# First router of a four-layer gated network: choosing four experts of sixteen with largest-eight and replace-first-match instructions per token tile

## The chip, the cores and the metric

One core of one Trainium2 chip. The metric is the device time of one execution in microseconds (us), as the median of several runs. Engines are called PE (TensorE, matrix multiplication), PEld (its weight loads), DVE (VectorE), ACT (ScalarE), POOL (GpSimd) and SP (SyncE, which here only issues DMA).

## The reference, cut to what matters

The network has four layers, each a cross-attention part and a feed-forward part, on 4 x 256 tokens of width 256. The change touches the router of the first layer's feed-forward part, a mixture of 16 experts in 4 groups. Per token, the two best groups are kept (a group's score is the sum of its two best biased scores), the four best experts in those groups are chosen, and their unbiased scores, normalised, become the weights:

```python
logits = x @ gate_weight.T
scores = jax.nn.sigmoid(logits)
biased = scores + expert_bias[None, :]
grp = biased.reshape(T, N_GROUP, gsz)                  # 4 groups of 4
top2, _ = jax.lax.top_k(grp, 2)
_, gidx = jax.lax.top_k(top2.sum(-1), TOPK_GROUP)      # 2 groups
gmask = jax.nn.one_hot(gidx, N_GROUP).sum(1)
masked = jnp.where(jnp.repeat(gmask, gsz, axis=1) > 0, biased, -jnp.inf)
_, sel = jax.lax.top_k(masked, TOP_K)                  # 4 experts
w = jnp.take_along_axis(scores, sel, axis=1)
w = w / (w.sum(-1, keepdims=True) + 1e-20) * SCALING
```

The experts' outputs (silu(x g) * (x u)) d are then summed with these weights, and a shared expert is added.

## The kernel before, in words

The 1024 tokens are 8 tiles (NT) of 128; a tile's tokens lie on the 128 partitions. All engines run programs of their own (the blocks at the end of `flamingo`), which meet at named semaphores. The order of the work is written out by hand; there is no planner. The stages are: the first state-space layer (`mamba0_*`), its tail, a layer norm (`ln_*`, k=1), the softplus that prepares the second state-space layer (`softplus_vector`, l=1), the first router (`router_*`, r=0), then one loop over the 8 token tiles in which the 17 units of the first mixture (`ffn_*`, f=0) are interleaved with the second state-space layer's scan (`mamba1_*`), then the ternary feed-forward part, the third layer's attention (`attn2_*`), an fp8 feed-forward part, the fourth attention, the second router and its experts.

Around the change:

- PE turns the normalised tokens (L328), ACT copies them to ZT (L336), PE multiplies them with the gate weights (L1058) and ACT takes the sigmoid (L1070) into `sc`, 128 x 128 (8 tiles of 16 experts).
- DVE meanwhile runs `softplus_vector` for l=1 (L457 to L481). Only behind it, in its own program's order, does it begin `router_vector`. Each of the router's instructions goes through `link`, which makes the instruction raise a semaphore and DVE wait for it before it starts the next.
- `router_vector` adds the bias (L1099), scores the groups (L1105 to L1113), picks two groups by the helper `top_k` with n=4 (the first of its two calls), writes a very low number (-3e38) over the experts of the other groups (L1118 to L1121), picks four experts by `top_k` with n=16 (the second call, with which the diff is concerned), and turns the chosen scores into the weights `cw` (L1123 to L1129). The last instruction raises `cw_done`.
- `top_k` compares all pairs: for every value it counts those that are larger, or equal and further in front, and takes the values whose count is below k. That is five instructions on 128 x (8 n n) elements: equal (L1084), times a mask (L1085), greater (L1086), add (L1087), reduce (L1089), and a comparison of the 8 n counts with k (L1090). For n=16 the five have 2048 elements per partition, for n=4 128.
- In `ffn_gpsimd` POOL waits for `cw_done`, then copies the first tile's tokens (L733) and weights (L737), and then starts the scan's products (`mamba1_drive`, L674). PE waits for these two copies before the first tile's matmuls (L782); ACT (L814) waits for PE, and DVE (L847, L850) for ACT. The same loop's scan on DVE is L643, its products with C are L651 and POOL's sums L681.
- SP has by then issued, in this order: the weights `gu0` and `dn0`, the ternary weights (L1969), the tables `moe` (L1970), `slot_scratch` (L1971, 4 MB), and the first four rows of the second scan (L350), which wait for nothing of the router. Further rows (L350) wait for the loop's own progress.

Of the kernel before, what the change touches and what calls it, by code (L numbers as in the profile page):

```python
# [7 lines left out]
ALU = mybir.AluOpType  # L8
# [11 lines left out]
NT = TOK // P  # L20
# [9 lines left out]
NEXP = 16  # L30
# [67 lines left out]
def flamingo(nc, a, out):  # L98
    with ExitStack() as ctx:
# [32 lines left out]
        def col(name):  # L132
            at, w = COL_AT[name]
            return cols[:, at:at + w]
# [155 lines left out]
        def S(name):  # L290
            if name not in sems:
                sems[name] = sem(name)
            return sems[name]
# [770 lines left out]
        sc, bi, sel, tmp1, tmp2, rank, grp, sm = (z[:, k * n_te:(k + 1) * n_te] for k in range(8))  # L1064
# [10 lines left out]
        def top_k(link, v, n, k, into):  # L1075

            a3 = v.rearrange("p (t i) -> p t i", t=NT)
            vi = a3.rearrange("p t (i o) -> p t i o", o=1).to_broadcast([P, NT, n, n])
            vj = a3.rearrange("p t (o j) -> p t o j", o=1).to_broadcast([P, NT, n, n])
            size = NT * n * n  # L1080
            c1 = cmp1[:, 0:size].rearrange("p (t i j) -> p t i j", t=NT, i=n)
            c2 = cmp2[:, 0:size].rearrange("p (t i j) -> p t i j", t=NT, i=n)
            before = jlti.rearrange("p (o i j) -> p o i j", o=1, i=NEXP)[:, :, 0:n, 0:n].to_broadcast([P, NT, n, n])
            link(nc.vector.tensor_tensor(c1, vj, vi, ALU.is_equal))  # L1084
            link(nc.vector.tensor_tensor(c1, c1, before, ALU.mult))  # L1085
            link(nc.vector.tensor_tensor(c2, vj, vi, ALU.is_gt))  # L1086
            link(nc.vector.tensor_tensor(c1, c1, c2, ALU.add))  # L1087
            rk = rank[:, 0:NT * n]
            link(nc.vector.tensor_reduce(rk.rearrange("p (t i) -> p t i", t=NT), c1, AX.X, ALU.add))  # L1089
            link(nc.vector.tensor_scalar(into, rk, float(k), None, ALU.is_lt))  # L1090

        def router_vector(dve, link, r):
            t3 = lambda v, n=NEXP: v.rearrange("p (t e) -> p t e", t=NT)
            nu = FFN[0 if r == 0 else 3]["units"]
            if r == 0:
                link(nc.vector.memset(cw[:], 0.5))
                dve.wait_ge(S("scores"), 1)
                eb = col("ebias").rearrange("p (o e) -> p o e", o=1).to_broadcast([P, NT, NEXP])
                link(nc.vector.tensor_tensor(t3(bi), t3(sc), eb, ALU.add))  # L1099

                g = bi.rearrange("p (q k) -> p q k", k=4)
                q4 = [g[:, :, k] for k in range(4)]
                n4 = n_te // 4
                m1, n1, m2, n2 = (tmp1[:, k * n4:(k + 1) * n4] for k in range(4))
                link(nc.vector.tensor_tensor(m1, q4[0], q4[1], ALU.max))  # L1105
                link(nc.vector.tensor_tensor(n1, q4[0], q4[1], ALU.min))
                link(nc.vector.tensor_tensor(m2, q4[2], q4[3], ALU.max))
                link(nc.vector.tensor_tensor(n2, q4[2], q4[3], ALU.min))
                link(nc.vector.tensor_tensor(n1, n1, n2, ALU.max))
                link(nc.vector.tensor_tensor(n2, m1, m2, ALU.min))  # L1110
                link(nc.vector.tensor_tensor(n1, n1, n2, ALU.max))
                link(nc.vector.tensor_tensor(m1, m1, m2, ALU.max))
                link(nc.vector.tensor_tensor(grp[:, 0:n4], m1, n1, ALU.add))  # L1113
                gsel = grp[:, n4:2 * n4]
                top_k(link, grp[:, 0:n4], 4, 2, gsel)

                em = gsel.rearrange("p (q o) -> p q o", o=1).to_broadcast([P, n4, 4])
                link(nc.vector.tensor_tensor(bi.rearrange("p (q k) -> p q k", k=4), g, em, ALU.mult))  # L1118
                link(nc.vector.tensor_scalar(grp[:, 2 * n4:3 * n4], gsel, 1.0, BIG, ALU.subtract, ALU.mult))
                pen = grp[:, 2 * n4:3 * n4].rearrange("p (q o) -> p q o", o=1).to_broadcast([P, n4, 4])  # L1120
                link(nc.vector.tensor_tensor(bi.rearrange("p (q k) -> p q k", k=4), g, pen, ALU.add))  # L1121
                top_k(link, bi, NEXP, 4, sel)
                link(nc.vector.tensor_tensor(tmp2, sc, sel, ALU.mult))  # L1123
                link(nc.vector.tensor_reduce(sm[:, 0:NT], t3(tmp2), AX.X, ALU.add))
                link(nc.vector.tensor_scalar(sm[:, 0:NT], sm[:, 0:NT], 1e-20, None, ALU.add))
                link(nc.vector.reciprocal(sm[:, NT:2 * NT], sm[:, 0:NT]))
                link(nc.vector.tensor_scalar(sm[:, NT:2 * NT], sm[:, NT:2 * NT], 0.5 * 2.5, None, ALU.mult))
                rc = sm[:, NT:2 * NT].rearrange("p (t o) -> p t o", o=1).to_broadcast([P, NT, NEXP])
                nc.vector.tensor_tensor(cw[:, :, 0:NEXP], t3(tmp2), rc, ALU.mult).then_inc(S("cw_done"), 1)  # L1129
# [951 lines left out]
        def _(dve):  # L2081
# [11 lines left out]
            softplus_vector(dve, link, 1)  # L2093
            dve.wait_ge(S("ld_w0"), 80)
            router_vector(dve, link, 0)
            ffn_vector(dve, 0, link)
            ln_vector(dve, link, 2)
# [125 lines left out]
```

## Time and profile before

| | us |
|---|---|
| median of 3 runs | 1041.7 |
| the runs | 1047.06, 1041.70, 1039.58 |
| the profiled execution, its own time | 1044.17 |
| its span in the profile | 1042.4 |
| mean granted TensorE clock in it | 0.869 of full |

The span is from the first to the last recorded instruction; the execution's own time is 1.8 us longer. In the profile an instruction is named by its line in the kernel (L1084), its engine, its operation, and output <- input by the program's names. PEclk is the TensorE clock that was granted, as a share of full speed.

### The profile page before, as it was taken

What the parts mean: (1) busy time and instruction counts of PE and PEld (TensorE: products, weight loads), DVE (VectorE), ACT (ScalarE), POOL (GpSimd) and SP (SyncE); (2) the same over time, 40 slices, a digit from 0 to 9 for tenths busy, and PEclk for the clock granted to TensorE, in tenths of its full rate; (3) what the DMA queues carried; (4) which work ended last, traced back from release to release, by engine and by line L of the source; (5) the groups of instructions that cost most, each with busy time, mean ns of one, the idle gap of its engine ahead of it and who ended that gap; (6) DMA issues with size and microseconds to landing.
All of it is one profiled execution on the core that took longest, in us unless ns stands there. A gap on an engine that the chain in (4) does not pass through costs nothing.

```text
span 1042.4 us, 12920 instructions
## 1 busy us (share of the span) xinstructions
PE 839.0 (80%) x4202; PEld 528.8 (51%) x4202; DVE 698.1 (67%) x1136; ACT 390.9 (37%) x824; POOL 417.0 (40%) x295
## 2 busy tenths in 40 slices
PE   5887898850688899888489887999884886979993
PEld 2332333340566777677377544555543675645661
DVE  5995999979788889888766554667845546412222
ACT  1433222340334444443255542465550531103331
POOL 4005666400466666666239602333520242232331
PEclk8985888975799999999789896899997996889997
DMA  5102212763022221221020011314126001051114
GB/s 206 45 1 108 74 60 81 282 219 88 0 81 81 81 81 43 78 80 40 0 72 1 31 61 40 119 33 134 34 65 221 12 1 61 22 189 64 46 49 149
DMA packets 28099, 81.67 MB, mean 78 GB/s; under 512 B 3313, under 2 KB 17153, under 8 KB 26529
## 3 DMA queue, kind: packets, MB, share of 16 engines
q1 hardware_dynamic: 25648, 73.25, 20.7%
q0 software_dynamic: 2256, 6.18, 1.7%
q10 hardware_dynamic: 144, 1.57, 0.4%
q8 instruction: 31, 0.51, 0.2%
q14 instruction: 20, 0.16, 0.1%
HBM read 65.64 MB, written 17.35 MB: 80 GB/s over the span
## 4 chain that ended last, share of the span: by engine, by line
PE 47%; DVE 18%; issue 15%; POOL 11%; DMA 3%; ACT 3%; SPq 1%; DVEq 0%; POOLq 0%; ACTq 0%
PE ps L511 6%; POOL M L674 4%; PE ps L1686 4%; PE ps L1327 4%; PE ps L1690 3%; PE ps L390 3%; PE ps L504 3%; PE ps L1728 3%; PE ps L894 2%; DVE M L643 2%; POOL ZT L977 2%; PE ps L1346 2%; DVE M L651 2%; POOL slot_scratch L1212 1%; PE ps L1604 1%
## 5 line engine op out<-in xcount | busy, mean ns | idle before, releaser
L782 PE MATMUL ps<-W,F 128*128 128x256 f32 x544 | 152.3, 406 | 54.4 <-POOL F L737 33.0
L782 PEld LDWEIGHTS ps<-W,F 128*128 128x128 f32 x544 | 103.2, 199 | 86.6 <-DVE W L850 39.5
L585 POOL TENSOR_TENSOR M<-M 128x1024 f32<-128x1024 f32 x32 | 75.2, 2352 | 100.6 <-DVE M L465 53.6
L681 POOL TENSOR_TENSOR W<-W,M 128x1024 f32<-128x1024 f32 x32 | 75.4, 2356 | 84.5 <-DVE M L651 84.5
L1757 ACT ACTIVATE N<-ps 128x512 f32<-128x512 f32 x128 | 69.5, 595 | 86.6 <-PE ps L1690 86.6
L814 ACT ACTIVATE F<-ps 128x128 f32<-128x128 f32 x136 | 37.7, 277 | 149.7 <-PE ps L782 149.6
L643 DVE TENSOR_TENSOR_SCAN M<-ps,M 128x512 f32<-128x512 f32 x64 | 78.0, 1219 | 21.4 <-POOL M L674 21.4
L1686 PE MATMUL ps<-M,W 32*128 32x256 f32 x512 | 78.8, 443 | 16.3 <-DVE W L1784 11.1
L1778 DVE TENSOR_REDUCE W<-ps 128x4 f32<-128x1024 f32 x64 | 78.1, 1221 | 12.5 <-PE ps L1690 9.2
L769 PE MATMUL ps<-W,F 128*128 128x256 f32 x272 | 83.8, 391 | 0.0
L1690 PE MATMUL ps<-W,M 32*128 32x256 f32 x512 | 83.8, 424 | 0.0
L511 PE MATMUL ps<-M,ident 128*128 128x512 f32 x128 | 75.0, 740 | 5.6 <-DVE M L610 5.6
L601 DVE TENSOR_TENSOR_SCAN M<-ps,M 128x1024 f32<-128x1024 f32 x32 | 73.3, 2290 | 8.4 <-ACT ps L556 5.3
L674 POOL TENSOR_TENSOR M<-N,M 128x1024 f32<-128x1024 f32 x32 | 74.9, 2349 | 0.0
L1686 PEld LDWEIGHTS ps<-M,W 32*128 32x128 f32 x512 | 47.5, 205 | 44.6 <-DVE W L1784 25.0
L556 ACT ACTIVATE ps<-M 128x1020 f32<-128x1020 f32 x32 | 35.7, 1115 | 81.7 <-DVE M L601 81.7
L894 PE MATMUL ps<-N_rounded,W_rounded 128*128 128x512 f32 x224 | 56.4, 397 | 3.2 <-DVE N_rounded L878 3.2
L1420 POOL DMA_INDIRECT ytok_scratch<-Z,M x31 | 29.7, 958 | 71.7 <-ACT Z L1382 71.7
L967 POOL TENSOR_TENSOR M_rounded<-Z,M_rounded 128x512 fp32r<-128x512 f32 x28 | 40.4, 1445 | 43.1 <-ACT M_rounded L944 43.1
L1690 PEld LDWEIGHTS ps<-W,M 32*128 32x128 f32 x512 | 56.2, 197 | 2.7 <-issue 1.2
L511 PEld LDWEIGHTS ps<-M,ident 128*128 128x128 f32 x128 | 28.6, 235 | 53.1 <-issue 42.2
L1399 DVE COPY M<-ps 128x128 f32<-128x128 f32 x31 | 9.1, 292 | 66.0 <-PE ps L1337 66.0
(279 smaller groups left out, 1723.8 us busy)
## 6 DMA issues: line engine op xcount, KB each, us to landing
M<-dbl_scratch SPq DMA_DIRECT2D x48, 512.0 KB, 4.0
W<-in_gu SPq DMA_DIRECT2D x1, 4800.0 KB, 16.2
W<-in_gu SPq DMA_DIRECT2D x1, 4352.0 KB, 14.4
att_scratch<-W SPq DMA_DIRECT2D x32, 128.0 KB
slot_scratch<-in_slots SPq DMA_DIRECT2D x1, 3999.0 KB, 18.7
M<-slot_scratch SPq DMA_DIRECT2D x3, 1032.0 KB, 9.4
W<-in_gu SPq DMA_DIRECT2D x2, 1536.0 KB, 6.9
W<-in_dn SPq DMA_DIRECT2D x1, 2176.0 KB, 19.1
```

Source lines behind the costliest of these rows:

```text
L511: last = nc.tensor.matmul(ps[:, 2 * t + half, :], ident[:], hC[:, t, half * HALF:(half + 1) * HALF], start=(n == 0), stop=True, skip_group ...
L585: nc.gpsimd.tensor_tensor(dBu[:, t, :], du[0][:, t, :], Bb[:, par, :], ALU.mult).then_inc(S("dBu_rdy"), 1)
L601: nc.vector.tensor_tensor_scan(hst[:, t, :], dAp, dBu[:, t, :], 0.0, ALU.mult, ALU.add).then_inc(S("h_rdy"), 1)
L643: nc.vector.tensor_tensor_scan(hst[:, t, at], dAp1[:, at], dBu[:, t, at], 0.0, ALU.mult, ALU.add).then_inc(S("h1_rdy"), 1)
L674: nc.gpsimd.tensor_tensor(dBu[:, t, :], du[1][:, t, :], Bb[:, par, :], ALU.mult).then_inc(S("dBu1_rdy"), 1)
L681: nc.gpsimd.tensor_tensor(u[1][:, t, :], u[1][:, t, :], hC[:, t, :], ALU.add).then_inc(S("y1_acc"), 1)
L769: last = nc.tensor.matmul(ps[:, YBANK[par], 0:DIM], hT[0:k, c % 4, :], dn[0:k, c, :], start=(c == 0), stop=(c == nch - 1))
L782: last = nc.tensor.matmul(up, ztt[:, par, c, :], gu[:, c, s, :], start=(c == 0), stop=(c == DC - 1))
L894: last = nc.tensor.matmul(ps[:, 4 + 2 * kind + q % 2, :], gu[:, c, u, kind * P:(kind + 1) * P], part[:, c, half * HALF:(half + 1) * HALF], ...
L1686: return nc.tensor.matmul(ps[:, b, q * SEQ:(q + 1) * SEQ], qst[32 * b:32 * b + 32, h, q * P:(q + 1) * P], kst[32 * b:32 * b + 32, h, :], s ...
L1690: return nc.tensor.matmul(ps[:, 4 + n % 3, k * SEQ:(k + 1) * SEQ], kst[32 * b:32 * b + 32, e, k * P:(k + 1) * P], qmax[32 * b:32 * b + 32, ...
L1778: nc.vector.tensor_reduce(spots[:, 2 * which:2 * which + 2], ps[:, 2 * which:2 * which + 2, :].rearrange("p b (q k) -> p b q k", q=2), AX. ...
```

## The change

The second call of `top_k` (n=16, k=4) goes. In its place DVE finds, for each of the 8 token tiles, the eight largest of the 16 scores (`max`, output in falling order, in `best`). After the last of them one memset overwrites the fifth to eighth of each with 2.5e38, which no score equals. Then, for each tile, `match_replace` looks for the eight numbers of `best` among the 16 scores and writes 3.0e38 over the first place at which each is found, into `tmp1`. A comparison with 3.0e38 gives `sel`. Within each group of eight instructions there is no wait; DVE waits after the last max, after the memset, after the last match_replace and after the comparison. The group router's `top_k` (n=4) and everything else stay.

```diff
+        TAKEN, NEVER = 3.0e38, 2.5e38
...
-                top_k(link, bi, NEXP, 4, sel)
+                best = rank[:, 0:8 * NT].rearrange("p (t k) -> p t k", t=NT)
+                for t in range(NT):
+                    last = nc.vector.max(best[:, t, :], t3(bi)[:, t, :])
+                link(last)
+                link(nc.vector.memset(best[:, :, 4:8], NEVER))
+                for t in range(NT):
+                    last = nc.vector.match_replace(t3(tmp1)[:, t, :], best[:, t, :], t3(bi)[:, t, :], TAKEN)
+                link(last)
+                link(nc.vector.tensor_scalar(sel, tmp1, TAKEN, None, ALU.is_equal))
```

## Rows read from the trace of the kernel before

**Rows 1.** The page: span, busy time, slices, and the chain that ended last.

```profile
span 1042.4 us, 12920 instructions
PE 839.0 (80%) x4202; PEld 528.8 (51%) x4202; DVE 698.1 (67%) x1136; ACT 390.9 (37%) x824; POOL 417.0 (40%) x295
...
PE 47%; DVE 18%; issue 15%; POOL 11%; DMA 3%; ACT 3%; SPq 1%; DVEq 0%; POOLq 0%; ACTq 0%
```

**Rows 2.** Waits, 235 to 269 us: engine, line, waited for, total us, times, longest.

```profile
POOL F L733 <- DVE F L1129: 42.4, 1, 42.4
...
PE ps L782 <- POOL F L737: 33.0, 1, 33.0
```

**Rows 3.** Timeline 225 to 300 us: start, duration, engine, line, operation, shape.

```profile
254.37 2.29 DVE L1084 TENSOR_TENSOR M<-Z 128x2048 f32<-128x2048 f32 x1
256.69 2.29 DVE L1085 TENSOR_TENSOR M<-M,F 128x2048 f32<-128x2048 f32 x1
...
263.67 2.29 DVE L1089 TENSOR_REDUCE Z<-M 128x128 f32<-128x2048 f32 x1
265.99 0.23 DVE L1090 TENSOR_SCALAR Z<-Z 128x128 f32<-128x128 f32 x1
...
267.55 0.29 DVE L1129 TENSOR_TENSOR F<-Z 128x128 f32<-128x128 f32 x1
268.02 0.39 POOL L733 COPY F<-ZT 128x256 f32<-128x256 f32 x1 [42.40 <-DVE F L1129]
...
268.61 5.32 PE L782 MATMUL ps<-W,F 128*128 128x256 f32 x12 [33.02 <-POOL F L737]
```

**Rows 4.** Chain that ended last, by line, 247 to 272 us.

```profile
by line: POOL M L674 18.4%; DVE M L1084 10.4%; DVE M L1087 10.4%; DVE M L1085 10.4%; DVE M L1086 10.4%; DVE Z L1089 10.4%; issue 6.3%; DVE N L465 4.9%; DVE Z L1090 1.7%; POOL F L733 1.6%; DVE Z L1099 1.2%; DVE F L1129 1.2%; DVE Z L1123 1.2%
```

**Rows 5.** Stretches: window, length, busy (x) of PE, PEld, DVE, ACT, POOL, PEclk, DMA share, GB/s.

```profile
244.00:248.00 4.00, 0.00 (x0) 0.00 (x0) 3.86 (x5) 0.00 (x0) 0.00 (x0) 0.50 0.14 58
...
256.00:260.00 4.00, 0.00 (x0) 0.00 (x0) 3.93 (x3) 0.00 (x0) 0.00 (x0) 0.50 0.00 0
...
268.00:272.00 4.00, 3.39 (x8) 2.71 (x9) 0.64 (x2) 1.20 (x2) 3.98 (x4) 0.50 0.00 0
...
276.00:280.00 4.00, 3.98 (x20) 3.08 (x20) 3.89 (x10) 2.07 (x7) 0.79 (x1) 1.00 0.00 0
```

**Rows 6.** Groups of DVE instructions: one small one by line, and a run of eight.

```profile
222.90 0.64 DVE L309 BATCH_NORM_AGGREGATE mv<-stats 128x2 f32<-128x6 f32 x8
...
L309 DVE BATCH_NORM_AGGREGATE mv<-stats x56: 146/149/183, 13.1 to 876.5; 128x2 f32<-128x6 f32 x56
...
L481 DVE MEMSET ps<- x1: 62/62/62, 248.8 to 248.8; 128x4 f32 x1
L1096 DVE MEMSET F<- x1: 178/178/178, 249.0 to 249.0; 128x144 f32 x1
...
L1111 DVE TENSOR_TENSOR Z<-Z 128x32 f32<-128x32 f32 x1 | 0.2, 193 | 0.0
```

**Rows 7.** Groups of instructions of the whole span: busy us, mean ns of one.

```profile
L1804 DVE RECIPROCAL M<-M 128x256 f32<-128x256 f32 x8 | 14.0, 1745 | 18.7 <-DMA M<-att_scratch 18.7
L1784 DVE TENSOR_TENSOR W<-ps,W 128x256 f32<-128x256 f32 x32 | 13.5, 423 | 28.3 <-PE ps L1718 28.3
```

**Rows 8.** Timeline of DVE in the third layer's attention: one L1784 per round.

```profile
636.54 0.42 DVE L1784 TENSOR_TENSOR W<-ps,W 128x256 f32<-128x256 f32 x1 [1.09 <-PE ps L1718]
642.55 0.42 DVE L1784 TENSOR_TENSOR W<-ps,W 128x256 f32<-128x256 f32 x1 [2.15 <-PE ps L1718]
...
659.54 0.42 DVE L1784 TENSOR_TENSOR W<-ps,W 128x256 f32<-128x256 f32 x1 [2.38 <-PE ps L1718]
663.48 0.43 DVE L1784 TENSOR_TENSOR W<-ps,W 128x256 f32<-128x256 f32 x1 [0.95 <-PE ps L1718]
```

**Rows 9.** Stretches there (columns as in rows 5).

```profile
639.00:642.00 3.00, 3.00 (x21) 1.60 (x15) 1.23 (x1) 1.15 (x3) 0.00 (x0) 0.50 0.00 0
...
660.00:663.00 3.00, 3.00 (x44) 1.91 (x40) 2.32 (x2) 1.44 (x4) 0.32 (x1) 1.00 0.02 7
```

## The prediction

> **What bounds the kernel now.** I began with the page, to see whether one engine is the bound: none is. PE is busy 80% of the span and makes 47% of the chain that ended last, DVE 18%, POOL 11% [rows 1]. So what a change is worth depends on its stage. Next I asked for the waits around the first router. Three engines stand still there. POOL waits 42.4 us, in one piece, for the router's last instruction (L1129), and PE waits 33.0 us for the copy that POOL makes behind it [rows 2]. ACT's next unit of the mixture needs PE. Nothing else than DVE runs: in the windows at 244, 256 us PE, ACT and POOL are at 0.00, and from 256 us the DMA moves nothing [rows 5]. The timeline then shows what DVE does in this hole. Behind the softplus of the second scan, which takes up to 249 us, it works through the router one linked instruction at a time. Five of them, on 2048 elements a partition, fill 254.37 to 265.99 us: L1084 to L1087 and L1089, at 2.29 us each [rows 3]. The chain confirms that they set the end: each of these five lines holds 10.4% of the stretch from 247 to 272 us, that is 2.6 us (2.3 us for the wide one, the rest for the narrow one of the group router) [rows 4]. The chance that any of this is hidden is therefore small.
>
> **What goes.** From the start of the wide L1084 (254.37) to the start of the comparison L1090 behind it (265.99) are 11.62 us [rows 3]: five times 2.29, and the gap of 0.03 us with which each linked instruction follows the last (256.69 - 254.37 - 2.29). The comparison stays in another form, one pass over 128 elements like L1090, 0.23 us [rows 3], so it cancels. The group router keeps its six narrow instructions.
>
> **What comes.** The trace has no max and no match_replace, so I price them by rows of small DVE instructions.
> - Price of an element: 128x32 takes 0.193 us [rows 6], 128x2048 takes 2.29 us [rows 3]; that is 2.10 us over 2016 elements, 1.04 ns each, and a fixed part of 0.16 us.
> - Price when several stand in a row without a wait, as here: eight of L309 take 0.64 us together, though one alone lasts 0.149 us [rows 6]. So they follow each other at (0.64 - 0.15) / 7 = 0.07 us: most of the fixed part overlaps.
> - Eight max: each reads 16 and writes 8 elements where L309 reads 6 and writes 2. I allow 0.02 us for that (16 elements at 1.04 ns): 7 x 0.09 + 0.17 = 0.80 us.
> - The memset writes 32 elements: between 0.06 us for 4 and 0.18 us for 144 [rows 6], 0.09 us.
> - Eight match_replace: the call must first take in eight values and then run over 16. I count two passes, 0.08 + 0.09 = 0.17 us: 7 x 0.17 + 0.26 = 1.45 us.
> - Three waits (after the last max, the memset, the last match_replace) at 0.03 us: 0.09 us.
>
> Sum 0.80 + 0.09 + 1.45 + 0.09 = 2.43 us, against 11.62: a gain of 9.2 us.
>
> The ends of that unknown. Below: match_replace is one pass and all run at L309's pace, 0.64 + 0.64 + 0.06 + 0.09 = 1.4 us, gain 10.2. Above: the dearest DVE arithmetic in the trace is the reciprocal, 1745 ns for 256 elements against 423 ns for a product of the same shape [rows 7], 5.2 ns more each. If the search for eight values went at 1.04 + 5.2 = 6.2 ns an element and nothing overlapped, an instruction on 16 elements would take 0.16 + 0.10 = 0.26 us; 24 of them and the memset and waits make 6.4 us, gain 5.2. I take the value near the lower end, because L309 is the nearest row: tiny, on the same engine, issued eight in a row without a wait.
>
> A rule that speaks against this: the Trainium skill, page "VectorE: DVE Perf Modes", section "The DRAIN you can't avoid", says that a DVE instruction starts only when the pipe behind the last is empty, that leaving out semaphores does not help, and that one should reduce the number of operations. This change raises the number. By that rule the eight L309 would have to take 8 x 0.149 = 1.2 us and take 0.64 [rows 6], so this trace does not bear it out for tiny instructions; the same page's section "Two Vector instructions with no wait between them" allows an earlier start, and counts match_replace as two instructions, which is what I had assumed. What the full price of each would give is worked out as a rival below from rows alone.
>
> **What is late next.** With cw ready 9.2 us earlier, at about 258.7 us, POOL's copies (L733), the scan's first product (L674) and PE's first matmul (L782) must find their other inputs. The tokens ZT and the gate products are done at 236 us, since PE stands still from then on (33.0 us before 268.61) [rows 2, 3]. The rows and weights that DMA brings are all issued before, wait for nothing of the router, and traffic is down to 58 GB/s in the window at 244 us and to 0 in the one at 256 us [rows 5]. No later DMA is issued until the loop asks for it. Apart from DVE I find nothing that is due between 249 us and 258 us, so the whole 9.2 us should reach the first matmul. The loop behind it is the same work and moves forward as a block; its rows are fetched on its own progress and move with it.
>
> The clock: PE begins the loop at half speed (1.2 GHz) in the window at 268 us and is at full speed (2.4 GHz) in the one at 276. It is at half speed already at 244 us, 8 us after PE's last work [rows 5]. A hole of 24 us in place of 33 therefore still ends at half speed, and the rise costs the same.
>
> **The sum.** The profiled execution took 1044.17 us (span 1042.4 [rows 1] and 1.8 outside it); 1044.17 - 9.2 = 1035.0 us. That execution lies 2.5 us above the median of the runs, 1041.7. The saving does not depend on that, so for a median I predict 1041.7 - 9.2 = 1032.5 us, 0.9% less. The three runs of before lie between 1039.6 and 1047.1, so a median of a few is good to some 3 us, and about 1% is what such a measurement can tell from no change. My forecast lies just inside it.
>
> **The rivals.**
> 1. *No overlap.* Each of the new instructions pays its whole 0.16 + 0.02 us: 24 x 0.18 + 0.18 = 4.5 us, gain 7.1, 1034.6 us. For it: max and match_replace need all eight comparisons finished, so they may not run into each other as L309's do. Against: L309's spacing [rows 6]. Chance 0.20.
> 2. *The clock falls elsewhere, to our good.* The moments at which TensorE's clock drops in later stages move with the work. In the third layer's attention a round (L1784 to L1784) takes 642.55 - 636.54 = 6.01 us at half speed and 663.48 - 659.54 = 3.94 us at full speed [rows 8, 9]. If the three slow rounds there went at full speed, 6.2 us more would be gained: 1026.3 us. The spread of the runs of before, 7.5 us, says that something of this size happens anyway. Chance 0.17.
> 3. *The clock falls elsewhere, to our harm, and it is slower.* The same mechanism, the other way: each further round at half speed in that attention costs 2.07 us. From 9.2 / 2.07 = 4.4, so five more slow rounds, the gain is gone; with nine it is 18.6 - 9.2, 1051.1 us. For it: there are 32 rounds, and most now run at full speed. Against: it needs some 30 us more at half speed in a stage in which PE hardly pauses once it has the full clock, and the work ahead of it is the same. Chance 0.03.
> 4. *Another wait takes the router's place.* A row of the scan or a table lands later than I read it, and POOL or PE still starts near 268 us: 1041.7 us. Rows 5 speak against it (no traffic at 256 us). Chance 0.04.
> 5. Forecast, overlapping small instructions with the later stages as they are: 0.56.
>
> **How the numbers follow.** The likeliest is 1032.5 us. The unknown price puts it between 1031.5 (gain 10.2) and 1036.5 (gain 5.2); the median's own uncertainty widens this to some 1029 and 1039, and rival 2 pulls the lower end down to 1027. Range 1027 to 1039. Faster by over 1% means below 1031.3: about a quarter of the forecast's 0.56, nearly all of rival 2, a little of rival 1, 0.34 together. Slower by over 1%: rival 3, 0.03. Within 1%: the rest, 0.63.
>
> **What would show it right or wrong.** In the profile of the changed kernel: the lines of `top_k` appear once each, in the narrow form only; the stretch between the write of the low numbers and the product with the scores is about 2.4 us plus the comparison (over 4 us: rival 1; over 11 us: the prices are wrong altogether); PE's single wait for POOL's copy falls from 33.0 to about 24 us, and POOL's from 42.4 to about 33; the first L782 starts near 259.4 us, still at half clock; the four double tiles of the loop keep their length. The prediction is wrong if PE waits for a DMA or for ACT at the head of the loop, or if the stages behind it take a different time by more than 2 us; then the granted clock of their windows is where to look.

## The result, and the profile after

| | before | after |
|---|---|---|
| median, us | 1040.68 (6 runs) | 1031.42 (6 runs) |
| profiled execution, own time | 1044.17 | 1031.28 |
| its span | 1042.4 | 1029.5 |

The ratio is 0.9906, with a 95% interval of 0.988 to 0.9932: faster by 0.9%. The forecast was 1032.5 us in 1027 to 1039.

The page of the changed kernel, top lines (they answer to [rows 1]):

```profile
span 1029.5 us, 12940 instructions
PE 833.1 (81%) x4202; PEld 527.1 (51%) x4202; DVE 689.3 (67%) x1156; ACT 391.0 (38%) x824; POOL 417.1 (41%) x295
```

DVE has 20 instructions more (1156 against 1136) and 8.8 us less work: 6 went, and 26 came: 8 max, a memset, 8 pairs for match_replace and a comparison. PE, ACT and POOL have as many instructions as before.

The timeline of the changed kernel from the last instruction in front of the selection to the head of the loop (start, duration; it answers to [rows 3]):

```profile
249.41 0.29 DVE L1123 TENSOR_TENSOR Z<-Z 128x128 f32<-128x128 f32 x1
249.73 0.71 DVE L1126 MAX8 Z<-Z 128x8 f32<-128x16 f32 x8
250.52 0.09 DVE L1128 MEMSET Z<- 128x32 f32 x1
250.64 0.09 DVE L1130 MATCH_VALUE_LOAD Z<-Z 128x8 f32 x1
250.72 0.16 DVE L1130 MATCH_REPLACE8 Z<-Z 128x16 f32<-128x16 f32 x1
250.79 0.08 DVE L1130 MATCH_VALUE_LOAD Z<-Z 128x8 f32 x1
...
251.73 0.16 DVE L1130 MATCH_REPLACE8 Z<-Z 128x16 f32<-128x16 f32 x1
251.92 0.23 DVE L1132 TENSOR_SCALAR Z<-Z 128x128 f32<-128x128 f32 x1
...
253.48 0.29 DVE L1139 TENSOR_TENSOR F<-Z 128x128 f32<-128x128 f32 x1
253.95 0.39 POOL L733 COPY F<-ZT 128x256 f32<-128x256 f32 x1 [32.97 <-DVE F L1139]
...
254.54 5.49 PE L782 MATMUL ps<-W,F 128*128 128x256 f32 x12 [21.29 <-POOL F L737]
...
257.02 0.29 DVE L847 SCALAR_TENSOR_TENSOR F<-F,ps 128x128 f32<-128x128 f32 x1 [3.25 <-ACT F L814]
...
259.80 1.22 DVE L643 TENSOR_TENSOR_SCAN M<-ps,M 128x512 f32<-128x512 f32 x1
```

Eight max take 0.71 us together, and the match_replace of one tile begins 0.14 us behind that of the tile before ((251.73 - 250.72) / 7). The first max begins at 249.73 and the comparison at 251.92: 2.19 us stand where 11.62 us stood [rows 3]. Everything behind keeps its length: the first product of POOL waits for the same copies, and PE's first matmul follows the router's last instruction by 1.06 us in both (254.54 - 253.48; 268.61 - 267.55 [rows 3]).

The waits of the changed kernel from 235 to 262 us (they answer to [rows 2]):

```profile
POOL F L733 <- DVE F L1139: 33.0, 1, 33.0
...
PE ps L782 <- POOL F L737: 21.3, 1, 21.3
```

Stretches of the changed kernel, columns as in [rows 5]:

```profile
252.00:256.00 4.00, 1.46 (x4) 1.19 (x5) 1.56 (x7) 0.00 (x0) 2.05 (x3) 0.50 0.00 0
256.00:260.00 4.00, 4.00 (x11) 2.88 (x10) 1.39 (x5) 3.02 (x5) 3.09 (x2) 0.50 0.00 0
260.00:264.00 4.00, 4.00 (x19) 3.19 (x18) 3.93 (x8) 1.96 (x7) 0.00 (x0) 0.91 0.00 0
```

POOL's wait is 9.4 us shorter, as the saving, and from 252 us on no DMA moves. PE starts the loop at half clock (0.50) and has the full one at 260.7 us (0.91 over the window at 260 us is 0.7 us at half clock and the rest at full), 6.2 us after its first matmul. In the two profiles of before this took 5.0 and 3.4 us; the loop is as long all the same (the table below).

**Where the whole difference lies.** The LayerNorm statistics (L305, the start of a LayerNorm) cut the span into parts; each number is the difference of two starts in one profile. `before_again`, `after_again` and `after_third` are second and third profiles of the same two kernels, told of below.

| part, us | before | before_again | after | after_again | after_third |
|---|---|---|---|---|---|
| start to the LayerNorm before the router | 220.2 | 214.8 | 215.5 | 215.8 | 215.0 |
| that LayerNorm to the first L782 | 48.5 | 48.5 | 39.0 | 39.0 | 39.0 |
| first L782 to the next LayerNorm (the loop) | 236.0 | 236.3 | 236.0 | 235.9 | 236.0 |
| the ternary part and the LayerNorms around it | 87.3 | 88.7 | 88.7 | 87.4 | 86.6 |
| third layer's attention, fp8 part | 212.7 | 214.2 | 212.8 | 208.0 | 214.1 |
| rest | 237.8 | 239.8 | 237.6 | 239.9 | 239.8 |

Only the second row differs between the kernels beyond what it differs within one: 48.47 against 39.03, 9.4 us. The loop is the same to 0.3 us in all five, and the other parts vary by 1 to 6 us from profile to profile of one kernel. So of the 12.9 us between the first two spans 9.4 belong to the change. The rest is luck, that is, profiles of one kernel differ by as much: 4.6 us ahead of the router, in code that both kernels share, of which 1.4 are given back in the ternary part.

### The profile page after: what moved, and what is told of

Its sections match the earlier page's. It is cut to its first block, busy times and chain, and to the rows that moved or that the text cites. A ratio compares the mean times of both kernels' runs of the same rounds, so it can differ in the third digit from the quotient of the medians.

```text
span 1029.5 us, 12940 instructions
## 1 busy us (share of the span) xinstructions
PE 833.1 (81%) x4202; PEld 527.1 (51%) x4202; DVE 689.3 (67%) x1156; ACT 391.0 (38%) x824; POOL 417.1 (41%) x295
## 4 chain that ended last, share of the span: by engine, by line
PE 44%; issue 21%; DVE 17%; POOL 10%; ACT 3%; DMA 3%; SPq 1%; DVEq 0%; POOLq 0%; ACTq 0%
PE ps L511 6%; POOL M L674 5%; PE ps L1696 4%; PE ps L1337 4%; PE ps L1700 4%; PE ps L390 3%; PE ps L504 3%; PE ps L1738 3%; PE ps L894 3%; DVE M L643 2%; POOL ZT L977 2%; PE ps L1356 2%; DVE M L651 2%; PE ps L1614 1%; PE ps L1354 1%
## 5 line engine op out<-in xcount | busy, mean ns | idle before, releaser
L782 PE MATMUL ps<-W,F 128*128 128x256 f32 x544 | 151.8, 404 | 43.2 <-DVE W L850 21.6
L782 PEld LDWEIGHTS ps<-W,F 128*128 128x128 f32 x544 | 102.3, 198 | 76.0 <-DVE W L850 40.9
L643 DVE TENSOR_TENSOR_SCAN M<-ps,M 128x512 f32<-128x512 f32 x64 | 78.0, 1219 | 21.4 <-POOL M L674 21.4
```

Source lines behind the costliest of these rows:

```text
L643: nc.vector.tensor_tensor_scan(hst[:, t, at], dAp1[:, at], dBu[:, t, at], 0.0, ALU.mult, ALU.add).then_inc(S("h1_rdy"), 1)
L782: last = nc.tensor.matmul(up, ztt[:, par, c, :], gu[:, c, s, :], start=(c == 0), stop=(c == DC - 1))
```

## The experiments

Medians are compared with those of before in the same job (1040.9 to 1041.8 us); "stage" is the time from the LayerNorm in front of the router to the next one behind the loop, 284.5 us in before and 275.0 us in after.

**1. The changed kernel again** (`after_again`, no edit).

> The changed kernel once more, beside the other three of this group. Both theories expect the router stretch (first LayerNorm statistics L305 behind the first layer to the first L782) to last 39.0 us as in the first profile, against 48.5 us before. Theory (the router is on the path, microsecond for microsecond): the time lies 9.4 us under before. Rival (part of the difference is a luckier clock in stages that the change does not touch): the stretch repeats to 0.1 us, while the parts ahead of it and behind it move by 1 to 5 us from profile to profile.

1029.71 us against 1041.17, ratio 0.9896 (0.9879 to 0.9914). The stretch is 39.0 us, so the router's gain repeats to 0.1 us. The time lies 11.5 us under before, 2 more than the stretch gives, and in this profile the attention and fp8 part took 208.0 us, 4.8 less than in the first one. The granted clock shows where: in the third layer's attention TensorE came back to full speed 10 us earlier. The window from 624 us, first in `after`, then in `after_again`:

```profile
624.00:628.00 4.00, 3.74 (x30) 2.77 (x31) 2.56 (x3) 1.34 (x3) 0.00 (x0) 0.50 0.00 0
624.00:628.00 4.00, 4.00 (x49) 2.26 (x42) 2.90 (x4) 2.17 (x4) 0.00 (x0) 1.00 0.00 0
```

Three rounds (L1784, here L1794) took 6.01, 10.87 and 6.15 us in `after` and 3.88, 8.90 and 5.41 us here, 4.8 us less together, which is the whole difference of that part. This is the mechanism of the prediction's second rival. It came in one of the thirteen profiles of these experiments (the other twelve have 211.3 to 214.2 us for the part), and not in the other two of this kernel, so the change alone does not bring it.

**2. Work of the same length put back** (`filled_before`).

```diff
                 best = rank[:, 0:8 * NT].rearrange("p (t k) -> p t k", t=NT)
+                for _k in range(4):
+                    link(nc.vector.tensor_tensor(cmp1, cmp2, cmp2, ALU.add))
                 for t in range(NT):
                     last = nc.vector.max(best[:, t, :], t3(bi)[:, t, :])
```

> Four additions on 2048 elements (results unused) stand in front of the max instructions, 4 x 2.32 = 9.3 us of DVE, each with a wait. Theory (path): PE's and POOL's first instruction of the loop start 9.3 us later, and the whole time goes back to that of before, +9.3 us over the changed kernel. Rival (the gain came from the clock or from how the instructions lie in the program): the time stays within 3 us of the changed kernel's.

1041.36 us, ratio to before 1.0012 (0.999 to 1.0033): the whole gain is gone. The stretch to the first L782 is 266.9 - 218.6 = 48.3 us, 9.3 over after, and the stage 284.7, 9.7 over after. The router is on the path microsecond for microsecond; the clock or the place of the instructions in the program did not make the 9.4 us of the stretch. In this job the medians differ by 2 us more than the stretch does, for before and for this kernel alike (11.5 and 11.7 us over `after_again`).

**3. The same work behind the hand-over** (`filled_behind`).

```diff
                 nc.vector.tensor_tensor(cw[:, :, 0:NEXP], t3(tmp2), rc, ALU.mult).then_inc(S("cw_done"), 1)
+                for _k in range(4):
+                    link(nc.vector.tensor_tensor(cmp1, cmp2, cmp2, ALU.add))
```

> The same four additions, but behind the instruction that hands over the weights, so PE, ACT and POOL start their head of the loop at once and DVE alone is 9.3 us late. Theory (the router's end matters through a hand-over in which DVE then waits 3.25 us for ACT, and 1.5 us more before its first scan): DVE's delay hides these waits, and the cost is 9.3 - 3.25 - 1.5 = 4.5 us, at most 6. Rival (DVE alone is the bound of this stretch and order does not matter): +9.3 us, as when the additions stand ahead of the hand-over.

1041.38 us, ratio 1.0 (0.9987 to 1.0014), and the stage is 285.3 us, +10.3. My theory fell: the cost is the full one and a microsecond more. The timeline of this kernel shows what I had left out:

```profile
258.14 13.54 DVE L1141 TENSOR_TENSOR M<-M 128x2048 f32<-128x2048 f32 x4
258.40 2.28 POOL L733 COPY F<-ZT 128x256 f32<-128x256 f32 x1 [32.96 <-DVE F L1139]
260.64 2.25 POOL L737 COPY F<-F 128x17 f32<-128x17 f32 x1
262.85 6.69 POOL L674 TENSOR_TENSOR M<-N,M 128x1024 f32<-128x1024 f32 x2
262.94 3.78 PE L782 MATMUL ps<-W,F 128*128 128x256 f32 x8 [27.53 <-POOL F L737]
```

The four additions take 13.54 us, not 9.28, and POOL's two copies 2.28 and 2.25 us, not 0.39 and 0.19. One by one the additions take 2.29, 2.37, 4.47 and 4.31 us: each copy ends 0.1 to 0.3 us after one of the first two, each of the other two lasts about as long as a product on POOL and an addition together, and POOL's two products stretch from 4.64 to 6.69 us. The two engines shut each other out instruction by instruction. The new theory: it is the second input from SBUF (the memory in which this kernel keeps its tiles; the `ps` tiles lie in another, PSUM) that DVE and POOL can't both have. The next experiment tests it.

**4. The same length, with one input** (`behind_reduce`).

```diff
                 nc.vector.tensor_tensor(cw[:, :, 0:NEXP], t3(tmp2), rc, ALU.mult).then_inc(S("cw_done"), 1)
+                for _k in range(4):
+                    link(nc.vector.tensor_reduce(rank, cmp2.rearrange("p (i j) -> p i j", j=NEXP), AX.X, ALU.add))
```

> As the kernel with four additions behind the hand-over, where they took 13.5 us in place of 9.3 and POOL's two copies 2.3 us each in place of 0.4 and 0.2; here four reductions of 2048 elements (2.29 us each, one input from SBUF in place of two; results unused). Theory (a DVE instruction with two inputs from SBUF and a POOL instruction shut each other out, one with a single input doesn't): the copies take 0.4 and 0.2 us again, the four reductions 9.3 us, the first scan starts 9.3 - 3.25 - 1.5 = 4.5 to 6 us later than in the changed kernel, measured from the end of the router, and the stage from LayerNorm to LayerNorm grows by 4.5 to 6 us over 275.0. Rival (whatever DVE does in the hand-over costs in full, because PE at half speed is waiting for it): +9.3 us or more, as with the additions (+10.3).

Timeline of this kernel:

```profile
254.14 9.24 DVE L1141 TENSOR_REDUCE Z<-M 128x128 f32<-128x2048 f32 x4
254.40 0.39 POOL L733 COPY F<-ZT 128x256 f32<-128x256 f32 x1 [32.97 <-DVE F L1139]
254.75 0.19 POOL L737 COPY F<-F 128x17 f32<-128x17 f32 x1
254.90 4.65 POOL L674 TENSOR_TENSOR M<-N,M 128x1024 f32<-128x1024 f32 x2
254.99 3.78 PE L782 MATMUL ps<-W,F 128*128 128x256 f32 x8 [23.59 <-POOL F L737]
...
264.14 2.07 PE L782 MATMUL ps<-W,F 128*128 128x256 f32 x4 [5.37 <-DVE W L850]
264.58 1.22 DVE L643 TENSOR_TENSOR_SCAN M<-ps,M 128x512 f32<-128x512 f32 x1
```

Copies, products and reductions all have their own length, though they lie side by side. The first scan starts 10.65 us after the router's last instruction (264.58 - 253.93), against 6.32 in after (259.80 - 253.48): +4.3 us, a little under the 4.5 expected. The median is 1036.83 us, ratio 0.9966 (0.9944 to 0.9987), and the stage 281.4 us, +6.4, a little over the 6 that the theory allowed. The other 2.1 us lie behind the first scan, and there the clock differs: while DVE reduces, PE stands still for 5.4 us after its first two units, the full clock comes and goes in this pause, and PE resumes at half speed. Windows of this kernel:

```profile
260.00:264.00 4.00, 0.00 (x0) 0.00 (x0) 3.90 (x4) 0.22 (x1) 0.00 (x0) 0.85 0.00 0
264.00:268.00 4.00, 3.86 (x10) 2.89 (x11) 3.17 (x7) 0.49 (x2) 0.00 (x0) 0.50 0.00 0
268.00:272.00 4.00, 4.00 (x18) 3.36 (x17) 2.84 (x7) 1.75 (x7) 0.00 (x0) 0.80 0.00 0
```

In after the scan starts at 259.80 with the full clock almost there (0.91 in the window at 260 us); here it comes 5.0 us behind the first scan. Experiment 8 sets such times against each other for seven profiles. Between this kernel and the last one the stage differs by 3.9 us (285.3 against 281.4), and that is the exclusion: beside POOL four additions last 4.3 us longer than four reductions.

The two kinds differ in a second way: an addition writes 2048 elements a partition, a reduction 128. So the output could be what they contend for. The loop of the changed kernel itself answers this:

```profile
267.25 1.22 DVE L643 TENSOR_TENSOR_SCAN M<-ps,M 128x512 f32<-128x512 f32 x1
267.44 2.37 POOL L674 TENSOR_TENSOR M<-N,M 128x1024 f32<-128x1024 f32 x1
268.95 1.41 DVE L651 TENSOR_TENSOR M<-M 128x512 f32<-128x512 f32 x1
```

The scan (L643) and the product (L651) both write 128x512, but the scan reads one input from PSUM (`ps`) and one from SBUF, the product both from SBUF. Beside a product on POOL each of 54 scans lasts 1.21 to 1.23 us, as the 10 that stand alone, and POOL's product keeps its 2.33 to 2.37 us; L651 goes from 0.68 to up to 1.41 us. A full output alone does not shut POOL out. That a port is what they contend for is inferred from these kinds of instruction; no run looked at the port itself.

The Trainium skill, page "SBUF — State Buffer", section "SBUF: two separate sides", says that DVE and GpSimd hold a shared port pair as a lock for a whole instruction, DVE where it runs in a two-port performance mode or, against a GpSimd instruction that reads SBUF, has two inputs from SBUF. This trace agrees (2.28 against 0.39 us for the copy).

**5. A wait behind each** (`linked`).

```diff
-                    last = nc.vector.max(best[:, t, :], t3(bi)[:, t, :])
-                link(last)
+                    link(nc.vector.max(best[:, t, :], t3(bi)[:, t, :]))
...
-                    last = nc.vector.match_replace(t3(tmp1)[:, t, :], best[:, t, :], t3(bi)[:, t, :], TAKEN)
-                link(last)
+                    link(nc.vector.match_replace(t3(tmp1)[:, t, :], best[:, t, :], t3(bi)[:, t, :], TAKEN))
```

> A wait after each of the eight max and eight match_replace, in place of one after the last. Theory (short DVE instructions overlap when no wait stands between them): from the start of the first max to the comparison 8 x (0.158 + 0.03) + 0.12 + 8 x (0.07 + 0.158 + 0.03) = 3.7 us in place of 2.19, so the stage grows by 1.5 us. Rival (an instruction starts only when the pipe is empty, whether or not a wait stands there): no change, 2.2 us.

Timeline of this kernel:

```profile
250.48 1.67 DVE L1126 MAX8 Z<-Z 128x8 f32<-128x16 f32 x8
252.22 0.09 DVE L1127 MEMSET Z<- 128x32 f32 x1
252.34 0.09 DVE L1129 MATCH_VALUE_LOAD Z<-Z 128x8 f32 x1
252.42 0.16 DVE L1129 MATCH_REPLACE8 Z<-Z 128x16 f32<-128x16 f32 x1
252.61 0.09 DVE L1129 MATCH_VALUE_LOAD Z<-Z 128x8 f32 x1
...
254.51 0.23 DVE L1130 TENSOR_SCALAR Z<-Z 128x128 f32<-128x128 f32 x1
```

The same eight max take 1.67 us in place of 0.71, and a match_replace comes every 0.27 us in place of 0.14. From the first max to the comparison are 4.03 us, +1.84, where the theory said 3.7 and the rival no change. The stage is 277.1 us, +2.1. Fourteen waits more than in after cost 1.84 us, 0.13 us each, and leaving them out is what makes the new selection 2.2 us long. The median, 1036.89 us (8 runs), lies 5.5 us over the first one of after. The stage explains 2.1 of them, and the profiled span (1031.6 us) is 2.1 us over that of after too. The rest goes with the clock: the three runs with a mean granted clock of 0.881 to 0.882 took 1032.8 to 1033.7 us, and the profile is one of them; the five with 0.873 to 0.874 took 1036.8 to 1037.8. Whether the waits bring the lower clock about more often or this was chance, eight runs don't show.

**6. Comparison with the fourth largest** (`threshold`).

```diff
-                link(nc.vector.memset(best[:, :, 4:8], NEVER))
-                for t in range(NT):
-                    last = nc.vector.match_replace(t3(tmp1)[:, t, :], best[:, t, :], t3(bi)[:, t, :], TAKEN)
-                link(last)
-                link(nc.vector.tensor_scalar(sel, tmp1, TAKEN, None, ALU.is_equal))
+                link(nc.vector.tensor_tensor(t3(sel), t3(bi), best[:, :, 3:4].to_broadcast([P, NT, NEXP]), ALU.is_ge))
```

> The four experts are those not below the fourth largest value: one comparison of the 16 scores with best[3] in place of the memset, the eight match_replace and the comparison with 3.0e38. Left out: the order among equal scores. Theory (path): memset to comparison, 250.52 to 252.18 = 1.66 us, become 0.32 us; the stage falls by 1.3 us against the changed kernel (275.0 to 273.7), the time by as much. Rival (the comparison's broadcast input or the later stages eat it): no change.

This kernel leaves out the choice among equal scores: if the fourth largest value occurs twice, it takes both. The stage is 273.7 us, 1.3 less, as expected. The median of 6 runs, 1031.26 us (ratio 0.9915, 0.9889 to 0.9941), can't show that: it lies among those of after (1029.71 to 1031.42).

**7. The router between the halves of the softplus** (`early`). DVE runs the whole router after the first of the softplus's two halves. What the loop's head needs is made ready there too, POOL waits for the first half (`du_done` 3) before it begins and for the second (4) only before its second product, and ACT waits for the first half as well.

```diff
-            softplus_vector(dve, link, 1)
             dve.wait_ge(S("ld_w0"), 80)
-            router_vector(dve, link, 0)
+            softplus_vector(dve, link, 1, lambda: router_vector(dve, link, 0))
...
+            if l:
+                dve.wait_ge(S("a_done"), l + 1)
+                nc.vector.tensor_scalar(Aneg, Aneg, -1.0, None, ALU.mult).then_inc(S("delta_done"), 1)
             for t in range(2):
+                if t:
+                    if l:
+                        dve.wait_ge(S("scores"), 1)
+                        nc.vector.memset(dAp1.rearrange("p (b l) -> p b l", b=BATCH)[:, :, 0:1], 0.0).then_inc(S("delta_done"), 1)
+                    between()
...
-            dve.wait_ge(S("a_done"), l + 1)
-            nc.vector.tensor_scalar(Aneg, Aneg, -1.0, None, ALU.mult).then_inc(S("delta_done"), 1)
+            if l == 0:
+                dve.wait_ge(S("a_done"), l + 1)
+                nc.vector.tensor_scalar(Aneg, Aneg, -1.0, None, ALU.mult).then_inc(S("delta_done"), 1)
...
-            else:
-                dve.wait_ge(S("scores"), 1)
-                nc.vector.memset(dAp1.rearrange("p (b l) -> p b l", b=BATCH)[:, :, 0:1], 0.0).then_inc(S("delta_done"), 1)
...
-            pool.wait_ge(S("du_done"), 4)
+            pool.wait_ge(S("du_done"), 3)
...
                     mamba1_drive(pool, t, 0)
+                    if first:
+                        pool.wait_ge(S("du_done"), 4)
                     mamba1_drive(pool, t, 1)
...
             act.wait_ge(S("delta_done"), 4)
+            act.wait_ge(S("du_done"), 3)
```

> The router moves between the two halves of the softplus, POOL begins with the first half's product, and ACT begins the loop as soon as the weights are there. The same work on DVE, in another order. Theory (what stands between the router's end and the first scan is the hand-over DVE to POOL to PE to ACT to DVE): the weights are ready about 10 us earlier, the first two units and the decays are made under the second half of the softplus, DVE's first scan starts 4.5 us earlier after the end of its own work, and the time falls by 3 to 4.5 us against the changed kernel. Rival (PE, cold and stalled again after two units, is then later than before): no gain, within 1 us of the changed kernel.

Timeline of this kernel (its lines are 8 higher from the router on):

```profile
243.60 1.21 POOL L739 COPY F<-ZT 128x256 f32<-128x256 f32 x1 [22.67 <-DVE F L1147]
244.59 1.30 DVE L466 SCALAR_TENSOR_TENSOR M<-M 128x1024 f32<-128x1024 f32 x1
...
245.91 2.35 POOL L680 TENSOR_TENSOR M<-N,M 128x1024 f32<-128x1024 f32 x1
245.93 2.88 DVE L468 TENSOR_SCALAR M<-M 128x1024 f32<-128x1024 f32 x1
246.00 3.78 PE L790 MATMUL ps<-W,F 128*128 128x256 f32 x8 [12.81 <-POOL F L743]
...
256.52 2.07 PE L790 MATMUL ps<-W,F 128*128 128x256 f32 x4 [6.74 <-DVE W L858]
256.96 1.22 DVE L649 TENSOR_TENSOR_SCAN M<-ps,M 128x512 f32<-128x512 f32 x1
```

The head of the loop is done under the softplus, and the first scan starts 41.5 us behind the LayerNorm (256.96 - 215.46), against 44.3 in after: 2.8 us earlier, not 4.5. The exclusion again is enough for the missing part: POOL's product of 2.35 us holds back L468, which takes 2.88 us in place of 0.69, 2.2 us more. L468 has one input, but it goes through 1024 elements in 0.69 us where an addition needs 1.22, so it runs in a faster form; a reduction of 2048 takes 2.29 us. Of the 2.8 us only 1.4 reach the end of the stage (273.6 us). PE has stood still for 6.7 us and works at half speed behind it: 0.50 in the window from 256 to 260 us. The median, 1029.87 us, is level with the 1029.71 of `after_again` in the same job. By the medians the rival held (within 1 us of the changed kernel). The stage shows a gain, 1.4 us of the 3 to 4.5 that the theory expected, and that is below what the times can show.

**8. Both** (`early_threshold`).

> The router between the halves of the softplus and the comparison with the fourth largest together. The first alone shortened the stage from LayerNorm to LayerNorm by 1.4 us (275.0 to 273.6), the second is expected to give 1.3. Theory (both lie on DVE's path): 272.3 us for the stage, the time 2.7 us under the changed kernel. Rival (with the router in front, its length is hidden behind ACT or PE): 273.6 us as with the first alone.

Stage 272.6 us (487.65 - 215.10), near the 272.3 expected, but a second profile of the same kernel (experiment 9) has 273.4. From the LayerNorm to the first scan they agree to 0.01 us, 40.33 us, that is 1.2 us less than `early`: ahead of the scan the two changes nearly add up. Behind the scan they differ, and so does the clock there. The windows in which it rises, first `early_threshold`, then `early_threshold_again`:

```profile
256.00:260.00 4.00, 4.00 (x16) 3.12 (x15) 3.37 (x7) 0.93 (x4) 0.58 (x1) 0.70 0.01 2
260.00:264.00 4.00, 4.00 (x13) 3.08 (x12) 3.25 (x7) 0.98 (x4) 0.18 (x1) 0.55 0.00 0
```

A window whose clock rises once from 0.50 to 1.00 gives the moment of the rise: 258.4 us in the first (0.70 is 2.4 of 4 us at half), 263.6 us in the second. Set against the first scan (255.43 and 259.03 us):

| profile | at half clock behind the first scan, us | first scan to the next LayerNorm, us |
|---|---|---|
| before | 0.0 | 230.8 |
| after | 0.9 | 230.7 |
| early_threshold | 3.0 | 232.2 |
| early | 3.5 | 232.1 |
| filled_behind | 4.0 | 232.4 |
| early_threshold_again | 4.6 | 233.1 |
| behind_reduce | 5.0 | 232.8 |

Where the full clock comes 3 to 5 us behind the scan, the rest of the loop is 1.3 to 2.4 us longer than in before and after, roughly the more the later it comes; two profiles of one kernel lie 0.9 us apart by it. Median 1029.86 us, ratio 0.9899 (0.9881 to 0.9916).

**9. Three more profiles in one job** (`before_again`, `after_third`, `early_threshold_again`).

> The kernel before, profiled a second time. The part from the start to the LayerNorm in front of the router took 220.2 us in the first profile of before and 215.1 to 220.0 in the nine profiles of kernels with the same code there. If that part varies by itself, it may come out anywhere in 215 to 220, while the stage from LayerNorm to LayerNorm, 284.5 us, repeats to 0.3 us. If it belongs to the kernel, it is 220 again.

> The changed kernel, beside the early router with the comparison with the fourth largest. The stage from LayerNorm to LayerNorm 275.0 us; the time 9.5 us under before, by the stage alone 0.991 of it.

> The early router with the comparison with the fourth largest, once more, beside the changed kernel. Its stage was 272.6 us against 275.0. If the whole time follows the stage it lies 2.4 us under the changed kernel's; if later stages take it back, level with it, as the medians of the first comparison had it (1029.9 against 1029.7).

`before_again` (one run, 1043.92 us) came out at 214.8 us for the part ahead of the router, so the 220.2 of the first profile was not the kernel's. Its stage is 284.7 us, against 284.5. The timeline of before has one reason; the first profile, then the second:

```profile
77.69 5.81 PE L408 MATMUL ps<-ZT,M 8*128 8x512 f32 x8 [0.77 <-ACT ZT L429]
```

```profile
74.71 3.67 PE L408 MATMUL ps<-ZT,M 8*128 8x512 f32 x8 [0.77 <-ACT ZT L429]
```

The same eight matmuls, 2.1 us longer, with DVE waiting behind them. The granted clock falls to half at 79.0 us in the one and at 78.9 us in the other (0.88 and 0.86 over the window at 76 us, 0.50 behind it), but in the first profile the matmuls began 3.0 us later, so most of them ran at half speed; in the second they were done. Of the 3.0 us the input's DMA has 1.5 (first statistics at 10.3 against 8.8 us), and L390 in front took 17.0 against 16.4 us. `after_third`: 1030.67 us, ratio 0.9891 (0.9861 to 0.992), stage 275.0. `early_threshold_again`: 1030.05 us, 0.9885 (0.9862 to 0.9909), stage 273.4, where the first profile had 272.6. Over all jobs the changed kernel has 1030.9 us (18 runs), before 1041.2 (61 runs), and the early one with the threshold 1030.0 us (12 runs): the direction of the stage, but 0.8 us is less than one job's uncertainty.

## Why the prediction was right

**What bounds it.** Right. The hole in which PE, ACT and POOL wait for the router was the place, and `filled_before` shows that 9.3 us of DVE work there cost 9.3 us in the stretch.

**What goes.** 11.62 us, exactly; the narrow instructions of the group router are unchanged.

**What comes.** 2.19 us for my 2.43. Eight max with the wait behind them 0.79 (I had 0.83), memset with wait 0.12 (0.12), eight match_replace with wait 1.28 (1.48). The pace of L309, 0.07 us [rows 6], was the right row: unlinked max come every 0.08 us, the two halves of match_replace every 0.07 to 0.08. The largest miss is 0.2 us, my allowance for elements, which the overlap hides.

**The clock.** Right about what counts: PE starts the loop at half speed, and the loop keeps its length. "The rise costs the same" was not so in detail (6.2 us to full speed in after, 5.0 and 3.4 in the two profiles of before), but in none of the three did it cost anything. PE's wait fell to 21.3 us, not to 24. The gate product in front (L1058) took 6.98 us in this profile against 5.05, because the clock was at half speed all through it (0.50 in the window at 230 us, 0.83 in before), and ended 2.3 us nearer to the router's end. In before's second profile PE's wait was 30.7 us and not 33.0, so these 2.3 us belong to the profile and not to the change; under the softplus they cost nothing.

**What is late next.** Right: nothing was. The first L782 follows the router's end by 1.06 us in both.

**The sum.** 9.2 forecast, 9.4 in the profile, 9.3 us between the medians (1040.68 - 1031.42), and 10.3 to 11.5 in the two later jobs. The forecast of the time itself, 1032.5 us, is 1.1 us over the median of 1031.4: 1.0 of that is the starting point (1041.7 from three runs, 1040.7 from six).

**The rivals.** No overlap (gain 7.1): this trace denies it, and `linked` shows its price: with a wait behind each the selection takes 4.03 us, the gain would be 7.6 us. Clock elsewhere: parts move by 1 to 6 us from profile to profile of either kernel (the table above), and `after_again` had 4.8 us of just what rival 2 describes. The mechanism is real and the change alone does not bring it. It may be part of the 1 to 2 us that the later jobs show beyond the stretch; no run shows that. The prediction's last sign, that a difference of more than 2 us behind the router would prove it wrong, was therefore too narrow: `after_again` would have failed it with the same router. Another wait: none. The rule of the Trainium skill in "VectorE: DVE Perf Modes", "The DRAIN you can't avoid", that leaving out semaphores gains nothing, does not hold for instructions this short: 1.67 us against 0.71 for the same eight. Where the page and the run differ, the run decides. (The advice to reduce the number of operations, which the prediction puts into that section too, stands in the page's section "Rules for kernel authors".)

## What to carry to other kernels

Counting over all pairs costs n times n elements per token; for the best four of 16, a max and a match_replace do it in 0.27 us a tile (2.19 / 8) if no wait stands between the tiles, and the saving arrives in full where all other engines wait for this one. Price a run of short instructions by the spacing of a similar run in the trace, not by the duration of one. When the difference of two profiles is larger than the sum says, cut both spans at the same events before believing in a second cause, and look at the granted clock of the part that differs.

## What was not expected

DVE and POOL stop each other for whole instructions: an addition of two SBUF operands (2.29 us) stretches a 0.39 us copy on POOL to 2.28 us and is itself held up, a reduction with one operand is not, nor is a scan with one of its two inputs in PSUM (experiments 3 and 4); a product on POOL of 2.35 us makes a one-operand DVE instruction of 1024 elements (L468, 0.69 us) last 2.88 us in experiment 7, so one operand alone is no protection where the instruction runs at twice the pace of the others (read from this one instruction, in three profiles; no run varied it). Work that is moved beside an idle engine is therefore not free when the idle engine is the other of these two. And what is saved in a head where PE then pauses is given back in part as half-speed time: 2.8 us earlier at the first scan were 1.4 us at the end of the loop (the table in experiment 8).
